# Decoder layer on one core: gate/up weights of the feed-forward as three bf16 parts, the SiLU taken straight from PSUM

## What is computed

```python
xq = _ste(x, axis=-1)              # x: (4, 256, 256); round(x / s) * s, s = max|x| / 127 per token
w1q = _ste(w_gate_up, axis=-1)     # (1408, 256); a scale per output row
gate_up = jnp.einsum('bsh,oh->bso', xq, w1q)
gate, up = (gate_up[..., :I], gate_up[..., I:])
h = jax.nn.silu(gate) * up         # I = 704
hq = _ste(h, axis=-1)
return jnp.einsum('bsi,oi->bso', hq, _ste(w_down, axis=-1))
```

## Time and profile before

| | |
|---|---|
| median of 3 runs | 250.27 us (250.07 to 250.71) |
| the profiled execution | 251.69 us, of it 249.9 us span from first to last instruction |
| last scan stage instruction (`weigh(3, 7, 1)`) ends | 174.45 us of the span |
| first `mm3` of batches 0, 1, 2, 3 starts | 177.14, 193.21, 212.98, 230.86 us |
| DVE busy | 220.4 us, 88% |

### The profile page before, as it was taken

The page is one execution under the profiler, slowest core; times in us unless marked ns, Lnnn a source line. Parts: engine busy times, 40 slices in busy tenths (PEclk is TensorE's granted clock), DMA queues, the critical chain, the costliest instruction groups (busy, mean ns, idle before and its releaser), DMA issues.

```text
span 249.9 us, 2858 instructions
## 1 busy us (share of the span) xinstructions
PE 168.8 (68%) x676; PEld 98.6 (39%) x676; DVE 220.4 (88%) x419; ACT 144.7 (58%) x307; POOL 144.6 (58%) x174
## 2 busy tenths in 40 slices
PE   0187498898485497867577479649878768729434
PEld 0155364464141344443423335234545446415232
DVE  2759989999999989989999999989899997894861
ACT  4018537965859375675566787346456886535151
POOL 3540898485456499457599564761484827551442
PEclk9999689999959769799999999776999997975957
DMA  6985643365353234352354644000000000000003
GB/s 179 341 298 104 230 135 109 110 138 116 84 127 113 98 114 138 127 129 77 90 155 148 152 98 129 0 0 0 1 3 1 21 0 0 25 0 0 0 0 126
DMA packets 15103, 23.23 MB, mean 93 GB/s; under 512 B 1136, under 2 KB 6640, under 8 KB 15088
## 3 DMA queue, kind: packets, MB, share of 16 engines
q1 hardware_dynamic: 13792, 21.92, 30.7%
q10 hardware_dynamic: 1296, 1.15, 1.4%
HBM read 21.88 MB, written 1.18 MB: 92 GB/s over the span
## 4 chain that ended last, share of the span: by engine, by line
DVE 35%; issue 22%; PE 19%; ACT 7%; POOL 7%; DMA 5%; SPq 2%; POOLq 0%; DVEq 0%; ACTq 0%
DVE Q L1043 8%; PE pY L741 6%; DVE prod L1054 6%; DMA fs_t<-w_in_t 5%; PE Q L229 3%; DVE am L980 3%; PE Q L893 3%; PE pA L708 2%; DVE w L1212 2%; POOL drive L354 2%; DVE tf L1219 2%; POOL w L384 2%; PE pX L229 2%; PE pA L229 1%; ACT Q L498 1%
## 5 line engine op out<-in xcount | busy, mean ns | idle before, releaser
L354 POOL TENSOR_TENSOR drive<-du,bc 128x512 f32<-128x512 f32 x64 | 79.9, 1272 | 31.2 <-DVE Q L1043 27.0
L741 PE MATMUL pY<-prod,ident 128*128 128x512 f32 x128 | 69.1, 678 | 12.7 <-DVE prod L1054 7.5
L1043 DVE TENSOR_TENSOR_SCAN Q<-Q,drive 128x512 f32<-128x512 f32 x64 | 75.1, 1212 | 0.8 <-ACT Q L498 0.8
L498 ACT ACTIVATE Q<-delta,negA 128x255 f32<-128x255 f32 x128 | 54.8, 470 | 24.9 <-DVE Q L1043 24.4
L1054 DVE TENSOR_TENSOR prod<-Q,bc 128x512 f32<-128x512 f32 x64 | 41.2, 674 | 0.9 <-PE pY L741 0.9
L741 PEld LDWEIGHTS pY<-prod,ident 128*128 128x128 f32 x128 | 25.5, 215 | 41.0 <-issue 27.9
L384 POOL TENSOR_TENSOR w<-w 128x352 f32<-128x352 f32 x16 | 15.4, 974 | 12.4 <-DVE w L1212 12.3
L229 PE MATMUL Q<-ident,w 128*128 128x128 f32 x48 | 10.1, 374 | 14.0 <-ACT w L597 14.0
L301 POOL TENSOR_SCALAR ve<-mv 128x2 f32<-128x2 f32 x12 | 3.9, 325 | 25.0 <-DVE mv L971 24.9
L1212 DVE TENSOR_TENSOR w<-Q,ws 128x704 f32<-128x704 f32 x16 | 13.6, 880 | 0.8 <-PE Q L877 0.5
L229 PEld LDWEIGHTS Q<-ident,w 128*128 128x128 f32 x48 | 7.6, 191 | 16.1 <-ACT w L597 15.8
(11 more groups left out here) (154 smaller groups left out, 330.3 us busy)
## 6 DMA issues: line engine op xcount, KB each, us to landing
bc<-bc_dram SPq DMA_DIRECT2D x32, 512.0 KB, 4.8
w<-w_gate_up SPq DMA_DIRECT2D x1, 1408.0 KB, 9.6
x_sb<-x SPq DMA_DIRECT2D x4, 256.0 KB, 3.6
fs_t<-w_in_t SPq DMA_DIRECT2D x1, 1024.0 KB, 12.4
out<-x_sb ACTq DMA_DIRECT2D x8, 128.0 KB, 1.8
w<-w_down SPq DMA_DIRECT2D x1, 704.0 KB, 11.0
ctx_t<-w_out_t SPq DMA_DIRECT2D x1, 512.0 KB, 12.7
xproj<-xproj_t SPq DMA_DIRECT2D x1, 160.0 KB, 3.0
```

The lines of the kernel that those rows point to most:

```text
L354: pool.tensor_tensor(drive[:, s % 2, h], du[:, b, h].unsqueeze(1).to_broadcast([P, SPS, T]), bc[:, g % 4, 0].rearrange("p (n t) -> p n t", ...
L498: act.activation(decay[:, h, n, 1:T], delta[:, b, h, 1:T], ACT.Exp, scale=negA[:, h, k:k + 1]).then_inc(S["decay_ready"], 1)
L741: ins = pe.matmul(pY[:], ident[:], prod[:, s % 2, :, n, :], start=(s == 0 and n == 0), stop=False, skip_group_check=True)
L1043: dve.tensor_tensor_scan(hid[:, h].rearrange("p n t -> p (n t)"), decay[:, h].rearrange("p n t -> p (n t)"), drive[:, s % 2, h].rearrange( ...
```

## The change

- `restore_w1` (POOL, 11 instructions of 128x256) takes MAGIC off the rounded weight and multiplies it by its scale, in fp32. `turn_w1` transposes that. The fp32 value is then split exactly: `w1_hi` (ACT, pX to bf16, in place of `w1_group`), `w1_part` (DVE, 6 instructions: pX minus the first part, fp32, into w1_rest), `w1_mid` (ACT, 6: the second part), `w1_lo` (POOL, 6: the third). pX is freed for the next group by `w1_part`.
- `mm3` runs 12 matmuls a call instead of 4 (three parts, the same x3q_t), so gate and up come out already scaled by the weights' scale.
- `gate_up3`, `gated3`, `tanh3`, `open3`, `mm_ws1` and `out_ws1` are gone. `silu3` (ACT, 16 of 128x352) reads the gate from PSUM with the token's scale, `hidden3` (DVE, 16 of 128x352) multiplies the up sum in PSUM with it. `inv3` has two instructions instead of four.
- The expert's gate of batches 2 and 3 uses Silu on ACT instead of Tanh with `gate1` on DVE.
- All five orders are written anew. On DVE all `round_w1` and `round_w2` now stand ahead of the first scan, `max_x(2)` ahead of the last `weigh`, and `stats3(0)`, `max_ad(1)`, `norm3(0)`, `max3(0)`, `scale3(0)`, `inv3(0)` and `quant3(0)` behind it. On POOL `restore_w1` stands in groups: 1 to 4 with `prep_du(1)` ahead of `drive_step(0, 7, 1)`, 5 to 8 ahead of `drive_step(1, 2, 0)`; `w1_lo` 0 and 1 with `restore_w1(9)` ahead of `drive_step(1, 5, 1)`, 2 and 3 ahead of `drive_step(2, 3, 0)`, 4 and 5 (behind `norm2(2)`) ahead of `drive_step(3, 5, 0)`.

```diff
-        w1q_t = sb("w1q_t", [P, H, FO * P], BF16)
+        w1q_t = sb("w1q_t", [P, 3, H, FO * P], BF16)
+        w1_rest = sb("w1_rest", [P, 2, 512])
...
-        ws1 = sb("ws1", [P, 2, F])
...
+        sc3 = sb("sc3", [P, NB, JT])
...
+        sg = sb("sg", [P, JT, F])
...
-            def gated3(b, j, c):
...
+            def restore_w1(c):
+                pool.wait_ge(S["w1_odd" if c % 2 else "w1_even"], c // 2 + 1)
+                pool.tensor_scalar(w1[:, c], w1[:, c], -MAGIC, w1s[:, c:c + 1], ALU.add, ALU.mult).then_inc(S["w1_deq"], 1)
+            def w1_lo(i):
+                h, k = i // 3, i % 3
+                n = min(4, FO - 4 * k) * P
+                pool.wait_ge(S["w1_mid"], i + 1)
+                pool.tensor_tensor(w1q_t[:, 2, h, k * 512:k * 512 + n], w1_rest[:, i % 2, 0:n], w1q_t[:, 1, h, k * 512:k * 512 + n],
+                                   ALU.subtract).then_inc(S["w1_lo"], 1)
...
+            drive_step(0, 6, 1); drive_step(0, 7, 0); restore_w1(1); restore_w1(2); restore_w1(3); restore_w1(4)
+            prep_du(1); drive_step(0, 7, 1); drive_step(1, 0, 0); drive_step(1, 0, 1); drive_step(1, 1, 0)
...
-                act.activation(th[:], gu[:, 0], ACT.Tanh, scale=0.5).then_inc(S["th_ready"], 1)
+                if b < 2:
+                    act.activation(th[:], gu[:, 0], ACT.Tanh, scale=0.5).then_inc(S["th_ready"], 1)
+                else:
+                    act.activation(th[:], gu[:, 0], ACT.Silu).then_inc(S["th_ready"], 1)
...
-            def tanh3(b, j):
...
+            def silu3(b, j, c):
+                act.wait_ge(S["gu_mm"], 4 * b + 2 * j + c + 1)
+                act.activation(sg[:, j, c * CH:(c + 1) * CH], Q[:, 2 * c, 0:CH], ACT.Silu, scale=sc3[:, b, j:j + 1])\
+                   .then_inc(S["silu_ready"], 1)
...
+            def w1_hi(i):
+                h, k = i // 3, i % 3
                 n = min(4, FO - 4 * k) * P
-                act.activation(w1q_t[:, h, k * 512:k * 512 + n], pX[:, 0:n], ACT.Copy, bias=-MAGIC).then_inc(S["w1_out"], 1)
+                act.wait_ge(S["w1_turned"], i + 1)
+                act.activation(w1q_t[:, 0, h, k * 512:k * 512 + n], pX[:, 0:n], ACT.Copy).then_inc(S["w1_hi"], 1)
+            def w1_mid(i):
+                h, k = i // 3, i % 3
+                n = min(4, FO - 4 * k) * P
+                act.wait_ge(S["w1_out"], i + 1)
+                act.activation(w1q_t[:, 1, h, k * 512:k * 512 + n], w1_rest[:, i % 2, 0:n], ACT.Copy).then_inc(S["w1_mid"], 1)
...
+            prep_u(1, 0); prep_u(1, 1); round_w1(2); round_w1(4); round_w1(6); decay_step(0, 0, 0); prep_out(2)
+            prep_dt(1); decay_step(0, 0, 1); decay_step(0, 1, 0); decay_step(0, 1, 1); decay_step(0, 2, 0)
...
+            out_xbc(2); quant2(1); quant1w(2); out_y(3); quant3(0); unmagic2(1); unmagic1w(2); unmagic3(0)
+            out_dbc(1); tanh1(2); silu3(0, 0, 0); silu3(0, 0, 1); scale_ctx(2); smooth_a(2); silu3(0, 1, 0)
+            scale_w(3, 0); scale_w(3, 1); scale_x(3, 0); quant4(0, 0); silu3(0, 1, 1); scale_x(3, 1); quant2(2)
+            unmagic4(0, 0); quant4(0, 1); quant3(1); unmagic2(2); unmagic4(0, 1); unmagic3(1); out_dbc(2)
+            silu3(1, 0, 0); silu3(1, 0, 1); quant1x(3); silu3(1, 1, 0); quant1w(3); quant4(1, 0); silu3(1, 1, 1)
+            unmagic1x(3); unmagic1w(3); out_xbc(3); quant4(1, 1); tanh1(3); unmagic4(1, 0); store_out(0, 0)
+            unmagic4(1, 1); quant3(2); scale_ctx(3); smooth_a(3); unmagic3(2); quant2(3); unmagic2(3)
+            silu3(2, 0, 0); silu3(2, 0, 1); out_dbc(3); quant4(2, 0); silu3(2, 1, 0); silu3(2, 1, 1)
+            unmagic4(2, 0); quant4(2, 1); quant3(3); store_out(0, 1); unmagic4(2, 1); unmagic3(3); silu3(3, 0, 0)
+            silu3(3, 0, 1); store_out(1, 0); store_out(1, 1); silu3(3, 1, 0); quant4(3, 0); silu3(3, 1, 1)
+            quant4(3, 1); unmagic4(3, 0); unmagic4(3, 1); store_out(2, 0); store_out(2, 1); store_out(3, 0)
+            store_out(3, 1)
...
-                    pe.wait_ge(S["w1_out"], 6)
+                    pe.wait_ge(S["w1_lo"], 6)
                 for g in range(2):
                     for h in range(H):
-                        ins = pe.matmul(Q[:, 2 * c + g, 0:CH], x3q_t[:, h, j * P:(j + 1) * P],
-                                        w1q_t[:, h, g * F + c * CH:g * F + (c + 1) * CH],
-                                        start=(h == 0), stop=(h == H - 1))
+                        for part in range(3):
+                            ins = pe.matmul(Q[:, 2 * c + g, 0:CH], x3q_t[:, h, j * P:(j + 1) * P],
+                                            w1q_t[:, part, h, g * F + c * CH:g * F + (c + 1) * CH],
+                                            start=(h + part == 0), stop=(h + part == H + 1))
                 ins.then_inc(S["gu_mm"], 1)
...
-            def mm_ws1(k):
...
+            mm2(0); turn_q1x(2); back1w(2); sum_step(3, 6); back2(1); mm_xbc(2); sum_step(3, 7); skip_y(3)
+            turn_q2(1); turn_q1w(2); turn_y(3); turn_q3(0); mm_dbc(1); mm1(2); mm3(0, 0, 0); mm2(1); turn_y2(3)
+            mm3(0, 0, 1); mm3(0, 1, 0); back2(2); mm3(0, 1, 1); turn_qf(0, 0); back1x(3); back1w(3); turn_q2(2)
+            mm4(0, 0); turn_qf(0, 1); turn_q3(1); mm_dbc(2); mm4(0, 1); mm2(2); mm3(1, 0, 0); mm3(1, 0, 1)
+            mm3(1, 1, 0); mm3(1, 1, 1); turn_q1x(3); turn_q1w(3); mm_xbc(3); mm1(3); turn_qf(1, 0); turn_qf(1, 1)
+            mm4(1, 0); mm4(1, 1); turn_q3(2); back2(3); mm3(2, 0, 0); turn_q2(3); mm3(2, 0, 1); mm_dbc(3)
+            mm3(2, 1, 0); mm2(3); mm3(2, 1, 1); turn_qf(2, 0); mm4(2, 0); turn_qf(2, 1); turn_q3(3); mm4(2, 1)
+            mm3(3, 0, 0); mm3(3, 0, 1); mm3(3, 1, 0); mm3(3, 1, 1); turn_qf(3, 0); turn_qf(3, 1); mm4(3, 0)
+            mm4(3, 1)
...
                 dve.wait_ge(S["th_ready"], b + 1)
-                dve.scalar_tensor_tensor(th[:], th[:], 1.0, gu[:, 0], ALU.add, ALU.mult).then_inc(S["a1_ready"], 1)
+                if b < 2:
+                    dve.scalar_tensor_tensor(th[:], th[:], 1.0, gu[:, 0], ALU.add, ALU.mult).then_inc(S["a1_ready"], 1)
...
+                if b < 2:
+                    dve.wait_ge(S["a1_ready"], b + 1)
+                else:
+                    dve.wait_ge(S["th_ready"], b + 1)
...
                     dve.wait_ge(S["ad_back"], b)
-                dve.scalar_tensor_tensor(a_t[:], th[:], 0.5, gu[:, 1], ALU.mult, ALU.mult).then_inc(S["a_ready"], 1)
+                dve.scalar_tensor_tensor(a_t[:], th[:], 0.5 if b < 2 else 1.0, gu[:, 1], ALU.mult, ALU.mult).then_inc(S["a_ready"], 1)
...
-                dve.reciprocal(rc3[:], sc3[:]).then_inc(S["rc3_ready"], 1)
-                dve.tensor_scalar(hx[:, b], sc3[:], 0.5, None, ALU.mult).then_inc(S["hx_ready"], 1)
-                dve.scalar_tensor_tensor(k3[:, b], sc3[:], 0.5, sc3[:], ALU.mult, ALU.mult).then_inc(S["k3_ready"], 1)
-                dve.scalar_tensor_tensor(k3q[:, b], sc3[:], 0.5 / QMAX, sc3[:], ALU.mult, ALU.mult).then_inc(S["k3q_ready"], 1)
+                dve.reciprocal(rc3[:], sc3[:, b]).then_inc(S["rc3_ready"], 1)
+                dve.tensor_scalar(k3q[:, b], sc3[:, b], 1.0 / QMAX, None, ALU.mult).then_inc(S["k3q_ready"], 1)
...
-            def gate_up3(b, j, c):
...
-            def open3(b, j):
...
+            def hidden3(b, j, c):
+                dve.wait_ge(S["silu_ready"], 4 * b + 2 * j + c + 1)
+                dve.tensor_tensor(tf[:, j, c * CH:(c + 1) * CH], Q[:, 2 * c + 1, 0:CH], sg[:, j, c * CH:(c + 1) * CH],
+                                  ALU.mult).then_inc(S["hf_ready"], 1)
...
+                dve.tensor_tensor(rk[:, j:j + 1], rh[:, j:j + 1], sc3[:, b, j:j + 1], ALU.mult).then_inc(S["rk_ready"], 1)
...
+            def w1_part(i):
+                h, k = i // 3, i % 3
+                n = min(4, FO - 4 * k) * P
+                dve.wait_ge(S["w1_hi"], i + 1)
+                if i > 1:
+                    dve.wait_ge(S["w1_lo"], i - 1)
+                dve.tensor_tensor(w1_rest[:, i % 2, 0:n], pX[:, 0:n], w1q_t[:, 0, h, k * 512:k * 512 + n], ALU.subtract)\
+                   .then_inc(S["w1_out"], 1)
...
+            prep_stats(0); constants(); prep_norm(0); prep_stats(1); conv_first(); zeros(); prep_norm(1)
+            prep_stats(2); prep_bc(0); max_w1(0); max_w1(1); max_w1(2); max_w1(3); max_w2(0); max_w2(1)
+            prep_relu(0); scale_w12(); wmax_in(0); round_w1(1); round_w1(3); wmax_in(1); wmax_in(2); prep_norm(2)
+            prep_delta(0); wmax_in(3); round_w2(0); round_w2(1); du_first(); prep_bc(1); round_w1(5); round_w1(7)
+            round_w1(9); prep_stats(3); scan(0, 0, 0); scan(0, 0, 1); weigh(0, 0, 0); weigh(0, 0, 1)
...
+            weigh(3, 6, 1); expert_out(0); scan(3, 7, 0); scan(3, 7, 1); weigh(3, 7, 0); weigh(3, 7, 1); stats3(0)
+            max_ad(1); scale_ad(1); inv_ad(1); max_w(2); scale_w1(2); inv_w1(2); norm3(0); max3(0); scale3(0)
+            inv3(0); quant3(0); residual1(3); stats2(3); gate_up1(2); norm2(3); up1(2); expert_out(1); amax_a(2)
```

(14 more changed lines are left out.)

284 lines of the change are left out of this document (103 added, 181 removed).

## The result

The changed kernel took 256.69 us (median of 4 runs, 253.75 to 260.02) against 250.17 for the kernel before on the same chip: slower, by a ratio of 1.017 (95% interval 1.011 to 1.024). The ratios leave out executions over 1.5% above the fastest of their kernel and so can differ from the ratio of the medians; the profiled execution here, 258.53 us (256.7 of it span), is one of those, while the second profile of the same kernel (e0, 256.48 us) is not. The experiments ran on three other chips (e0 to e7 on one, e8 to e11 and e12 to e14 on two more); on the first of them the same kernel gave 1.0265 (1.0205 to 1.0325) beside 250.92. The forecast was 246.6.

The account below looks back on a forecast made before the run. DVE was taken to bound the scans and one batch's chain the last window; -1.4 + 3.6 + 1.2 - 4.1 - 1.5 - 1.5 = -3.7 gave 248.0 for the profiled execution, 246.6 us as the median, range 241 to 252.

Parts of the forecast that it names:

- My chains go by the full clock: Behind the scans: batch chains priced with TensorE at its full clock, denser matmuls expected to keep the clock up.
- What bounds the kernel: Whole kernel: scans are DVE's work with 3.5 us idle; in the last window one batch's chain sets the end.
- Ahead of the scans, +1.6: Before the first scan: roundings add 3.9 us, 2.4 fill a DMA wait, so the first scan comes at 29.4.
- The scan stage, -3.0: First scan to last weigh: roundings -3.9, w1_part +3.6, max_x(2) and small ones +0.9, work moved to the tail -3.6.
- so I cost it at nothing: Scan stage: 13.9 us of new POOL work taken as free, because POOL works up to two steps ahead.
- Up to the first mm3, +3.6: Last weigh to first mm3: 6.3 us instead of 2.7, for DVE work moved there, transposes and hops.
- Windows 1 and 2, 17.3 and 15.7: First two batch windows behind the scans: lengths in us, against 16.07 and 19.77 before (+1.2 and -4.1).
- the term for VectorE's queue: Window 1: DVE's queue from quant3(0) to quant3(1) ends 9.15 us behind the first mm3.
- the 0.8 for the load: Window 1: one ACT table load of 1.28 us for the first Silu, adding 0.8 us to the window.
- Windows 3 and 4, 16.4 and 17.5: Last two batch windows: lengths in us, against 17.88 and 19.04 before (-1.5 each).
- the first rival: Clock stays low in mm3: matmuls cost twice as much, a whole batch adds 7.1 us, 253.7 us; chance 0.15.
- VectorE's* sum alone: Tail: DVE's work falls from 59.0 to 46.0 us, but the saving doesn't come through whole; batch chains set later windows.

Follow-up runs that it names:

- e0: The changed kernel again, unaltered, for the spread and a second trace: ratio 1.0265 to the kernel before.
- e7: The edit in the kernel before's engine orders, each instruction replaced by what the edit puts for it: ratio 1.1009 to the kernel before.
- e8: Changed kernel, hidden3 waiting for the matmul alone and multiplying by a constant tile instead of the SiLU: ratio 1.0271 to the kernel before.
- e11: e7 with one bf16 part as in e9, so old orders without the split: ratio 1.013 to the kernel before.
- e12: One bf16 part, orders of the kernel before up to the first mm3 group, the changed kernel's behind it: ratio 1.0434 to the kernel before.
- e14: Changed kernel with three round_w1 and two round_w2 moved from ahead of the first scan into the scans: ratio 1.0202 to the kernel before.
- e2: Changed kernel without restore_w1 and w1_lo on POOL, second part used twice, still 12 matmuls a call: ratio 1.0196 to the kernel before.
- e9: Changed kernel with weights rounded to bf16 once, no w1_part, w1_mid, w1_lo, 4 matmuls a call: ratio 1.0032 to the kernel before.
- e5: Changed kernel with 3, 5 and 10 unread matmuls added on TensorE in the last windows to keep the clock up: ratio 1.0121 to the kernel before.
- e1: Changed kernel whose mm3 runs only the first of three parts (4 matmuls a call), all parts still made: ratio 1.0214 to the kernel before.
- e10: e9 with 39 unread matmuls in TensorE's idle stretches behind the scans: ratio 0.9918 to the kernel before.
- e4: Changed kernel with a one-column SiLU added, moving the table load into the end of the scans: ratio 1.0223 to the kernel before.
- e6: The kernel before with 62 unread matmuls in TensorE's idle stretches behind the scans: ratio 0.9864 to the kernel before.
- e13: e12 with 36 unread matmuls in TensorE's idle stretches behind the first window: ratio 1.0298 to the kernel before.

## Why the prediction was wrong

Two steps failed: the scan stage, in which POOL's new work was costed at nothing, and *"My chains go by the full clock"* for the last two windows. Together they are 6.4 of e0's 8.5 us.

- **What bounds the kernel**: held. Scans 97.7% VectorE (144.06 of 147.45), the last window one batch's chain.
- **Ahead of the scans, +1.6**: 29.5 in e0, 30.7 in the first profile. Three `round_w1` (L1281) took 2.83 us where the forecast had 3 x 0.46 = 1.4; two drives had begun at 26.86. e14 shows that it hardly matters.
- **The scan stage, -3.0**: failed, by 3.8 us in the first profile and 3.1 in e0. VectorE's busy time there rose by 0.9 instead of falling by 3.0, and its idle time is as before, 3.4 us. Without stretches its instructions add up to 2.8 less than before, as forecast, `w1_part` with 3.8 (forecast 3.6) in it. What they last above the shortest of their kind (by tile and shape, scans and weighs left out) adds up to 4.7 us before and 7.0 after: +2.3. This is what *"so I cost it at nothing"* had wrong, by its mechanism: POOL was never late with a drive, as I had argued; its instructions lengthen VectorE's. The remaining 1.4 is in the counting: instructions in a row overlap by 0.08 us in the trace, there are 13 fewer, and the overlaps fell from 17.9 to 16.5, so an instruction taken out gives back less than its duration.
- How strong this is: the single stretched instructions are in the trace. Their sum depends on where the small instructions fall as much as on POOL's work: 4.5 in e2 and 5.0 in e9 (without the split), but 7.2 in e0, 7.9 in e5, whose scan stage is no longer for it (145.7), and 3.7 in e7, where POOL has the same added instructions in other places. The stage itself varies from 145.4 to 147.5 over e0, e1, e4, e5, e8 and the first profile, whose scans are the same but for one SiLU. That the stretches cost the whole kernel 2.3 us is therefore an estimate from their sum; no run isolates it.
- The Trainium skill, page "SBUF — State Buffer", section "Who interferes with whom", says that a `tensor_scalar` in a two-port mode and GpSimd block each other for the whole instruction; the traces agree (1.19 and 1.40 us, ending within 0.2 us of the drive). I had quoted it and given it no term.
- **Up to the first mm3, +3.6**: measured +3.9. VectorE is busy for 6.03 of these 6.59 us: moved work.
- **Windows 1 and 2, 17.3 and 15.7**: 17.8 and 16.8. Neither matmuls (e10) nor table load (e4) make them. In the first the term for VectorE's queue was 1.8 too small and the 0.8 for the load was for nothing; in the second ScalarE's `silu3(1, 1, 1)` came 1.0 later than forecast. This is read from the trace; only e8's 0.5 us in window 2 tests it.
- **Windows 3 and 4, 16.4 and 17.5**: 17.8 and 19.6; *"My chains go by the full clock"* failed. With the clock up they are 16.75 and 17.44 (e5). That was the first rival, given 0.15 and priced at 7.1 us; it came at half that. I had argued from the earlier trace rows that the clock was low because PE had been idle, and that denser matmuls would cure it. They don't: the low stretch starts between two batches' `mm3`, where PE waits for ScalarE around a few transposes, and, where it lasts 6.8 us, the next 48 matmuls begin in it.
- The page "TensorE: Matmul & The Clock Gate" of the Trainium skill, section "HAM oscillation — how this bites in real kernels", lays half rate to idle gaps. Here the longest gap around the fall was 1.38 us and PE had worked between the gaps; the measurement decides.
- **The change as a whole**: the SiLU from PSUM and the new orders alone (e9) are worth nothing (1.0032, with 8.8 us less of VectorE's work: 211.6 for 220.4). The split costs 4.6 us (e9 against e1: 1.8% of 250), tripled matmuls with their clock some 1.3 to 3.
- **Where e9's saving went**: its windows 2 to 4 are 5.6 us shorter than before (51.1 for 56.7), but the first `mm3` of the second batch starts 5.2 us later (198.4 for 193.2). Work was moved ahead of the first scan and behind the last weigh, where it delays the start of the feed-forward: first scan +3.8, scan stage -4.2, up to `mm3` +3.9, window 1 +1.7. That *VectorE's* sum alone doesn't set the length of the last windows held as forecast.

Open: what the orders before the first `mm3` cost by themselves, which e12 was to tell and doesn't; the price of POOL's new work in time; and why the low stretch of the clock lasts 3.4 us in some executions and 6.8 in others.

## What to carry to other kernels

Work put on an engine that is full is paid in full (w1_part), work taken from one that waits is paid back as another wait (e8). Work moved out of a full stage is not gone: look at what it delays at its new place (e9). The engine named in the largest wait need not be the cause: take the wait away before believing it. An edit that adds an engine to a chain must be judged together with the orders of all queues; the same edit was 6.5 or 25 us slower. And look at the granted clock at the start of every dense stretch, not at its mean: matmuls that nobody reads were worth 1.0 to 1.4 points in four kernels (e5, e6, e10, e13), some 3 us, but an execution whose clock recovers in time (e14) has part of that without them.

## What the hardware showed unexpectedly

- The granted clock fell to 0.50 at 232 us with PE half busy and no gap over 1.38 us, and stayed there until about 239, though PE was busy for 3.8 of the 4 us up to 238. In e2 and e14, with the same matmuls, the low stretch at that place lasted 3.4 us.
- VectorE instructions of 4 elements a partition took up to 1.29 us (e5, at 159.73) beside a POOL instruction of 1.27, and 0.15 to 0.2 without.
- The first SiLU behind Exp took one table load of 1.28 us, and there was no other between Copy, SiLU and the roundings behind it.
